# A feed-forward stage with its operands exchanged: exact sign weights in two products, scale and bias per partition, and transposes back

## What is computed

```python
x = layernorm(x + attention(x, Wq, Wk, Wv))
w = (weights >= 0.0) * 2.0 - 1.0              # +1 or -1, 512 x 512
y = einsum('bsi,oi->bso', x, w)
y = clip(y * scale + bias, -100, 100)          # scale, bias: (512,)
x = layernorm(x + y)
```

## Time and profile before

| | |
|---|---|
| median of 3 runs | 2723.28 us (2723.14 to 2724.53) |
| the profiled execution | 2723.15 us |
| its span in the profile | 2721.4 us |
| PE busy | 2686.9 us (99%) |
| DVE busy | 2308.4 us (85%) |
| ACT busy | 2261.1 us (83%) |
| POOL busy | 341.1 us (13%) |

### The profile page before, as it was taken

The page is one execution under the profiler, slowest core; times in us unless marked ns, Lnnn a source line. Parts: engine busy times, 40 slices in busy tenths (PEclk is TensorE's granted clock), DMA queues, the critical chain, the costliest instruction groups (busy, mean ns, idle before and its releaser), DMA issues.

```text
span 2721.4 us, 76294 instructions
## 1 busy us (share of the span) xinstructions
PE 2686.9 (99%) x32088; PEld 1351.0 (50%) x32088; DVE 2308.4 (85%) x1983; ACT 2261.1 (83%) x2726; POOL 341.1 (13%) x342
## 2 busy tenths in 40 slices
PE   9999999999999999999999999999999999979998
PEld 8888888733333333333333333333333333337887
DVE  7444444389999999999999999999999999978998
ACT  5333333399999999999999999999999999965665
POOL 1000000000000000010000000000000000005665
PEclk9999999999999999999999999999999999989999
DMA  6555555557686777768677686867768677655553
GB/s 227 191 194 193 188 186 186 197 132 169 132 176 140 155 157 158 162 126 184 138 153 165 142 172 135 167 147 157 168 131 172 141 159 158 150 145 177 189 189 136
DMA packets 216706, 445.22 MB, mean 164 GB/s; under 512 B 15570, under 2 KB 130258, under 8 KB 189780
## 3 DMA queue, kind: packets, MB, share of 16 engines
q0 software_dynamic: 27504, 200.29, 37.4%
q1 hardware_dynamic: 179108, 222.61, 26.2%
q10 hardware_dynamic: 9792, 17.83, 1.7%
HBM read 122.43 MB, written 117.96 MB: 88 GB/s over the span
## 4 chain that ended last, share of the span: by engine, by line
ACT 48%; PE 31%; issue 16%; DMA 3%; DVE 2%; SPq 0%; DVEq 0%; POOL 0%; ACTq 0%; POOLq 0%
ACT probs L769 48%; PE banks L226 19%; PE banks L1007 7%; DMA total<-partial 2%; PE banks L632 1%; PE banks L996 1%; PE banks L661 1%; PE banks L989 1%; PE banks L1003 1%; DVE partial L818 1%; DVE total L821 0%; DVE partial L821 0%; PE banks L248 0%; PE banks L990 0%; PE banks L254 0%
## 5 line engine op out<-in xcount | busy, mean ns | idle before, releaser
L769 ACT ACTIVATE probs<-banks 128x1024 f32<-128x1024 f32 x2048 | 1877.7, 1457 | 3.9 <-PE banks L632 3.9
L632 PE MATMUL banks<-score_rows 97*32 97x512 f16 x16384 | 1117.4, 380 | 4.5 <-issue 4.0
L661 PE MATMUL banks<-probs,v_keys 128*32 128x512 f32 x8192 | 1060.5, 592 | 0.1
L821 DVE TENSOR_TENSOR partial<-partial,probs 128x2048 f32<-128x2048 f32 x384 | 879.4, 2290 | 33.4
L632 PEld LDWEIGHTS banks<-score_rows 97*32 97x32 f16 x16384 | 361.3, 95 | 708.2 <-ACT probs L769 484.3
L818 DVE TENSOR_TENSOR partial<-probs 128x2048 f32<-128x2048 f32 x192 | 439.6, 2290 | 23.6 <-ACT probs L769 16.7
L601 POOL DMA_DIRECT2D total<-partial x191 | 164.7, 862 | 1713.7 <-DMA total<-partial 703.3
L661 PEld LDWEIGHTS banks<-probs,v_keys 128*32 128x32 f32 x8192 | 249.0, 111 | 209.9 <-ACT probs L769 0.2
L821 DVE TENSOR_TENSOR total<-total,probs 128x2048 f32<-128x2048 f32 x128 | 292.6, 2286 | 6.8
L354 DVE TENSOR_TENSOR qk_lo<-banks,qk_hi 128x512 f16<-128x512 f32 x128 | 88.3, 690 | 241.6 <-ACT qk_hi L309 241.6
L680 PEld LDWEIGHTS banks<-total,ones 128*32 128x32 f32 x3584 | 105.6, 109 | 280.7 <-issue 265.1
(11 more groups left out here) (95 smaller groups left out, 2117.5 us busy)
## 6 DMA issues: line engine op xcount, KB each, us to landing
total<-partial POOLq DMA_DIRECT2D x191, 1024.0 KB, 8.3
scratch_q_raw<-qk_raw SPq DMA_DIRECT2D x16, 1024.0 KB, 5.7
scratch_k_raw<-qk_raw SPq DMA_DIRECT2D x16, 1024.0 KB, 5.7
scratch_v<-v_out SPq DMA_DIRECT2D x16, 1024.0 KB, 5.1
score_rows<-scratch_q_hi SPq DMA_DIRECT2D x128, 128.0 KB, 4.6
score_rows<-scratch_k_hi SPq DMA_DIRECT2D x128, 128.0 KB, 3.5
v_keys<-scratch_v SPq DMA_DIRECT2D x64, 256.0 KB, 5.8
scratch_attn<-wf_scaled SPq DMA_DIRECT2D x64, 256.0 KB
```

The source lines that it names most:

```text
L632: last = nc.tensor.matmul(scores_of(phase, unit)[part, i, :], k_rows[:, h, keys], q_rows[:, h, qb * BLK:(qb + 1) * BLK], start=True, stop= ...
L661: last = nc.tensor.matmul(banks[rows, out_bank(qb), :], v_keys[:, kt, rows], probs[:, kt % P_RING, h, :], start=(kt == 0), stop=(kt == KT ...
L769: nc.scalar.activation(probs[:, kt % P_RING, heads, :], scores_of(it % SLOTS, qb * UNITS + u), ACT.Exp, scale=SCALE / GAIN ** 2).then_inc( ...
L821: nc.vector.tensor_tensor(into, into, probs[:, kt % P_RING], ALU.add).then_inc(a_sum, 1)
```

## The change

The feed-forward product is turned round. The sign weights, which are exactly representable, become the stationary operand `wf`, unscaled and unsplit; the moving operand is `yT` of four tiles (512 tokens). One unit u is then one group of 128 output features for 512 tokens: four chunks times two parts, 8 products of 512 columns where there were 13. The result has features in partitions, so ScalarE applies scale and bias as a column each while it evicts (`linear`), GpSimd clips (`clipped`), and TensorE transposes each tile back with four transposes (lag `BACK` = 11), from which VectorE adds y (`res2`).

The lags grow to `LN1, TRANS, FFN, LINEAR, BACK, LN2 = 1, 2, 6, 7, 11, 12`, so that the 64 tiles take 76 steps. `y` gets 16 slots, in the room of the score rows. The denominators are no longer transposed tile by tile: three batches in 16 transposes at the start of the block, the last one in 16 more in step 5, with their reciprocals in groups (`reciprocal_of`). `std`, `rstd` and `offset` are made once for both normalisations of a step, `offset` now from two tensors. On TensorE a step is: transposes of `y` (j-2), of `attnT` (j), back (j-11), product (u = j-6). On VectorE it begins with `res2` (j-11). The stores of the output go to SyncE's queue. The first loads of the block (`den`, `attnT`, and now x) are issued ahead of the last item's stores. Loops written as hardware loops become unrolled. In `project` the scaled and split weights and the bias rows go away. Of the diff, cut to its core:

```diff
--- project
-                nc.vector.scalar_tensor_tensor(out=wf_scaled[:], in0=w_in[:, 3], scalar=-1.0,
-                                               in1=scale_b.unsqueeze(1).to_broadcast([P, DC, D]),
-                                               op0=ALU.add, op1=ALU.mult).then_inc(s_scaled, 1)
-                nc.vector.tensor_copy(bias_rows[0:1, :], bias_in[0:1, :]).then_inc(s_bias, 1)
-                nc.vector.tensor_copy(bias_rows[HD:HD + 1, :], bias_in[HD:HD + 1, :]).then_inc(s_bias, 1)
...
-                nc.vector.tensor_tensor(wf_lo[:], wf_scaled[:], wf_hi[:].bitcast(FP32), ALU.subtract).then_inc(s_wflo, 1)
+                nc.vector.tensor_scalar(wf[:], w_in[:, 3], -1.0, None, ALU.add).then_inc(s_sign, 1)
...
--- attend
-    out_sb, den_sb = wf_scaled[:, 0:2, :], wf_scaled[:, 2:4, :]
+    out_sb = sb("out_sb", [P, 2, BLK], FP32)
+    den_sb = sb("den_sb", [P, 2, BLK], FP32)
...
+        def first_loads():
             for h in range(2):
+                sp.wait_ge(a_store[h], LAST * QB // 2 * 32 + 32)
+            sp.dma_start(first.den[:], dram["den"][0:(N - 1) * H, :]).then_inc(first.s_den, 16)
+            sp.dma_start(first.attnT[:], dram["attn"][0, :, 0:BLK].rearrange("(c p) t -> p c t", p=P)).then_inc(first.s_attnT, 16)
+            sp.dma_start(first.x[:], x[0]).then_inc(first.s_x, 16)
...
+            first_loads()
             for qb in range(QB):
                 store(LAST, qb)
-            finish_stores()
...
--- normalise_and_ffn
-    ATTN, LN1, TRANS, FFN, CLIP, LN2 = 0, 1, 2, 4, 5, 6
+    LN1, TRANS, FFN, LINEAR, BACK, LN2 = 1, 2, 6, 7, 11, 12
+    STEPS = TILES + LN2
...
     def _(sp):
+        for j in range(STEPS + 1):
+            if j % TPB == 0 and 2 <= j // TPB + 1 < NBLK:
+                load(j // TPB + 1)
+            t = lagging(j - 1, LN2)
+            if t is not None:
+                sp.wait_ge(f_y[1], t + 1)
+                sp.dma_start(out[t], y2[:, t % 4]).then_inc(f_out[t % 4], 16)
...
     def _(pool):
-                nc.gpsimd.tensor_tensor(res2[:, s % 2], clipped[:, s % 2], y[:, s % Y_SLOTS], ALU.add).then_inc(f_res[1], 1)
+            u = lagging(j, LINEAR)
+            if u is not None:
+                q, o = divmod(u, DC)
+                pool.wait_ge(f_linear, u + 1)
+                if q >= 2:
+                    pool.wait_ge(f_back, (q - 1) * TPB)
+                nc.gpsimd.tensor_scalar(clipped[:, q % 2, o, :], linear[:, u % 2, :], -MAX_VAL, MAX_VAL, ALU.max,
+                                        ALU.min).then_inc(f_clip, 1)
...
     def _(pe):
+        pe.wait_ge(first.s_den, 16)
+        rows = (N - 1) * H
+        for kt in range(KT):
+            last = nc.tensor.transpose(banks[:, 4 + kt // 8, kt % 8 * rows:(kt % 8 + 1) * rows],
+                                       first.den[:, kt * P:(kt + 1) * P], ident3[0:rows, 0:rows])
+        last.then_inc(f_denT, 1)
+        for j in range(STEPS):
+            t = lagging(j, TRANS)
             if t is not None:
+                pe.wait_ge(f_y[0], t + 1)
+                if t >= 2:
+                    pe.wait_ge(f_ylo, t - 1)
                 for c in range(DC):
+                    last = nc.tensor.transpose(yT_bank(t)[:, c * P:(c + 1) * P], y[:, t % Y_SLOTS, c * P:(c + 1) * P], ident3[:])
+                last.then_inc(f_yT, 1)
+            t = lagging(j, 0)
...
+                    last = nc.tensor.transpose(aT_bank(t)[:, c * P:(c + 1) * P], attnT[k][:, c, cols], ident3[:])
+                last.then_inc(f_aT, 1)
+            t = lagging(j, BACK)
             if t is not None:
...
+                    pe.wait_ge(f_clip, (q + 1) * DC)
+                if t >= 2:
+                    pe.wait_ge(f_res[1], t - 1)
+                for o in range(DC):
+                    last = nc.tensor.transpose(back_bank(t)[:, o * P:(o + 1) * P], clipped[:, q % 2, o, cols], ident3[:])
+                last.then_inc(f_back, 1)
+            if j == FFN - 1:
+                pe.wait_ge(f_denlast, 16)
+                for kt in range(KT):
+                    last = nc.tensor.transpose(banks[:, 6, kt * H:(kt + 1) * H], den_last[:, kt * P:(kt + 1) * P],
+                                               ident3[0:H, 0:H])
+                last.then_inc(f_denT, 1)
+            u = lagging(j, FFN)
+            if u is not None:
+                q, o = divmod(u, DC)
...
+                if o == 0:
+                    pe.wait_ge(f_ylo, (q + 1) * TPB)
+                if u >= 2:
+                    pe.wait_ge(f_linear, u - 1)
                 for c in range(DC):
-                    for part, w in ((yT_hi, wf_hi), (yT_lo, wf_hi), (yT_hi, wf_lo)):
+                    for part in (yT_hi, yT_lo):
+                        last = nc.tensor.matmul(ffn_bank(u), wf[:, c, o * P:(o + 1) * P], part[:, q % 2, c, :],
+                                                start=(c == 0 and part is yT_hi), stop=(c == DC - 1 and part is yT_lo))
                 last.then_inc(f_ffn, 1)
...
     def _(act):
+            if u is not None:
+                o = u % DC
+                act.wait_ge(f_ffn, u + 1)
...
+                nc.scalar.activation(linear[:, u % 2, :], ffn_bank(u), ACT.Identity, scale=columns[:, 0, o:o + 1],
+                                     bias=columns[:, 1, o:o + 1]).then_inc(f_linear, 1)
...
+                nc.scalar.activation(std[:, j % 2, lanes], mean_var[:, j % 2, lanes, 1], ACT.Sqrt, bias=eps[:]).then_inc(f_std, 1)
+            t = lagging(j, LN1)
             if t is not None:
+                act.wait_ge(f_offset, j)
...
+                nc.scalar.activation(y[:, t % Y_SLOTS], res1[:, t % 2], ACT.Identity, scale=rstd[:, j % 2, 0:1],
+                                     bias=offset[:, j % 2, 0:1]).then_inc(f_y[0], 1)
...
     def _(dve):
+        for j in range(STEPS):
+            t = lagging(j, BACK)
             if t is not None:
+                dve.wait_ge(f_back, t + 1)
...
+                nc.vector.tensor_tensor(res2[:, t % 2], back_bank(t), y[:, t % Y_SLOTS], ALU.add).then_inc(f_res[1], 1)
+            norms = norms_at(j)
+            for which, t in norms:
+                dve.wait_ge(f_res[which], t + 1)
+                nc.vector.bn_stats(stats[:, j % 2, which], (res1, res2)[which][:, t % 2]).then_inc(f_stat[which], 1)
...
+                nc.vector.reciprocal(rstd[:, j % 2, lanes], std[:, j % 2, lanes]).then_inc(f_rstd, 1)
+                dve.wait_ge(f_rstd, j)
+                nc.vector.scalar_tensor_tensor(out=offset[:, j % 2, lanes], in0=mean_var[:, j % 2, lanes, 0], scalar=-1.0,
+                                               in1=rstd[:, j % 2, lanes], op0=ALU.mult, op1=ALU.mult).then_inc(f_offset, 1)
...
```

More of the change, by code:

```diff
@@ L62, in project @@
 def project(nc, ctx, dram, args, banks, ffn, early):
-    xT, WT, WfT, scale, bias = args
-    wf_hi, wf_lo, bias_ones, bias_rows, wf_scaled = ffn
+    xT, WT, WfT, scale_bias = args
+    wf, columns = ffn
     rows16, v_keys, v_out = early.rows16, early.v_keys, early.v_out
@@ L154, in _ @@
         sp.dma_start(w_in[:, 3], WfT).then_inc(s_wf, 16)
-        sp.dma_start(scale_b, scale.partition_broadcast(P)).then_inc(s_ffn, 16)
-        for row in (0, HD):
-            sp.dma_start(bias_in[row:row + 1, :], bias.partition_broadcast(1)).then_inc(s_ffn, 16)
+        sp.dma_start(columns[:], scale_bias).then_inc(s_columns, 16)
         for b in range(NBLK):
@@ L546, in _ @@
             store(LAST, QB - 1)
-            finish_stores()
+            for h in range(2):
+                sp.wait_ge(a_store[h], ITEMS * QB // 2 * 32 + 32)
+            first_loads()
         with sp.Else():
@@ L588, in _ @@
                                 pattern=[[-1, P]], channel_multiplier=1).then_inc(m_id, 1)
-        pool.wait_ge(a_const, 1)
-        nc.gpsimd.memset(first[1][:], 0.0).then_inc(a_const, 4)
         pool.sem_inc(m_max, 2)
@@ L863, in normalise_and_ffn @@
     mean_var = sb("mean_var", [P, 2, 2, 2], FP32)
-    std = sb("std", [P, 2, 2, 1], FP32)
-    rstd = sb("rstd", [P, 2, 2, 1], FP32)
-    offset = sb("offset", [P, 2, 2, 1], FP32)
+    std = sb("std", [P, 2, 2], FP32)
+    rstd = sb("rstd", [P, 2, 2], FP32)
+    offset = sb("offset", [P, 2, 2], FP32)
     f_const = sem("f_const")
-    f_den = sem("f_den")
-    f_in = [first[2], sem("f_in1")]
-    f_x = [sem(f"f_x{k}") for k in range(2)]
+    f_denlast = sem("f_denlast")
+    f_denT = sem("f_denT")
+    f_rden = sem("f_rden")
+    f_in = [first.s_attnT, sem("f_in1")]
+    f_x = [first.s_x, sem("f_x1")]
     f_aT = sem("f_aT")
-    f_rden = sem("f_rden")
     f_attn = sem("f_attn")
@@ L1009, in step @@
                 last.then_inc(f_ffn, 1)
-        all_steps(pe, step)
     @block.scalar
     def _(act):
-        act.sem_inc(f_y[0], 2)
-        act.sem_inc(f_y[1], 2)
-        def deviation(t, s, which):
-            act.wait_ge(f_stat[which], (t + 1) * 2)
-            act.wait_ge(f_rstd[which], (t + 1) * 2)
-            nc.scalar.activation(std[:, s % 2, which], mean_var[:, s % 2, which, 1:2], ACT.Sqrt, bias=eps[:]).then_inc(f_std[which], 1)
```

(27 more changed lines are left out.)

343 lines of the change are left out of this document (146 added, 197 removed).

## The result

The median is **2900.7 us** (4 runs, 2898.8 to 2901.5) against 2723.2 us before (4 runs): ratio 1.0646, interval 1.0633 to 1.0659. The profiled execution's span is 2899.5 us. It is slower, as forecast, and inside the range, but 36 us above the predicted 2865.

The account below looks back on a forecast made before the run. TensorE was taken to bound the kernel at 4.02 us a tile. Start to 2489.6, 55 loop steps of 5.58 us (307) and the end gave 2827 us at full clock; 38 for alternating clock made 2865, range 2815 to 2985.

Parts of the forecast that it names:

- The loop: Last stage, each step: offset, ScalarE's y, TensorE's three transpose groups, VectorE's res2 to the next offset, in 55 steps.
- The 5.58 us: Length of one turn of the loop at full clock, summed from its members, against 4.02 us a step before.
- The likeliest case: TensorE's clock alternates, half of the time at each level: 6.27 us a step, 2865 us, chance 0.40.
- The 0.69 us for the clock: Step's lengthening by alternating clock, from 5.58 to 6.27 us; fully at the low level it would be 1.38.
- 38 us were put down for the clock: Last stage: the alternating clock adds 38 us to the full-clock 2827 us, giving 2865.
- The rival "`offset` behind GpSimd's addition": VectorE's two-tensor offset waits for GpSimd's res1: 1.27 us a step more, 2909 us at full clock; chance 0.26.
- The race of 0.04 us: After attn starts, GpSimd's res1 would start at 0.77 us and VectorE's offset at 0.81; first to start decides.
- The start: Last stage before the full loop: TensorE starts at 2442.64, den transposes 3.5 us, reciprocals 0.7; ends at 2489.6.
- At nothing, under the exponentials: Attention stage: issuing the first loads ahead of the last item's stores was costed at nothing, hidden under the exponentials.
- The clip: GpSimd's clip of 512 elements, with no row to size it, taken as 1.29 us like its addition.
- VectorE alone, 2.4 a step: End of the last stage: ten steps without transposes of y, 2.4 us each on VectorE with std between, 24 us.
- The rival on the other side: If y reaches TensorE in time, no loop: VectorE's 3.5 us sets the step, 2713 us; chance 0.06.

Follow-up runs that it names:

- e12: Changed kernel with offset made by one tensor-and-column operation per normalisation and every feed-forward product made twice: 2841.7 us, 5.60 us a step.
- e2: Changed kernel with TensorE's step reordered: transposes back first, then of attnT, then of y, then the product: 2816.9 us.
- e1: Changed kernel with offset made, as before the change, by one operation of a tensor and a column for each normalisation: 2848.0 us.
- e4: Changed kernel with each feed-forward product made twice into the same bank, the second overwriting the first: 2878.9 us.
- e5: Changed kernel with the first loads of den, attnT and x issued behind the last item's four stores instead of ahead: 2901.6 us.
- e9: e8 with the three first loads issued one by one, each ahead of one of the last three stores: 2735.0 us.
- after: The kernel with the whole change and no follow-up edit, against the kernel before: 2900.7 us, ratio 1.0646.
- e8: e3 with four slots for res2 in place of two: 2735.7 us.
- e10: e9 with GpSimd's addition res1 ahead of its clip in each step: 2768.1 us.
- e3: Changed kernel with the edits of both e1 and e2, offset by columns and transposes back first: 2782.6 us.
- e13: e10 with transposes back and the last normalisation each a step later (lags 12 and 13): 2711.8 us.
- e7: Kernel before the change with eight products instead of twelve, the weights' low part left out: 2705.7 us.
- e11: e10 with 8 unread products of 512 columns added in each of steps 1 to 5 of the last stage: 2765.5 us.

## Why the prediction was right, and where it was off

**The loop: right.** The chain has its members in the predicted order, VectorE's `res2` is released by the transposes back and TensorE's transposes by `y`. The 5.58 us were 5.60 in `e12`, at full clock and without a held `offset`, and opening the loop (`e2`) took 84 us off. The terms one by one, from the turn shown: `res2` to `attn` 2.02 (2.10 predicted), `attn` to `rstd` 0.59 (0.61), `rstd` to `offset` 0.19 (0.20), `y` and the wait of TensorE 0.86 (0.87), the transposes until `res2` 1.57 (1.49).

**The likeliest case: its kind right, its size off, and a rival missing in it.** The clock did alternate, but less: it was 0.85 and not the 0.75 of half and half. In 23 of the 52 steps from 12 to 64 the transposes of the loop ran at the low level (17 of these steps took over 7.7 us, 5 behind a free `offset` 6.57 to 6.72, the last 6.87), and a step at the low clock cost 1.28 more and not 1.38. The 0.69 us for the clock were 0.54, and 0.23 in the version in columns (`e1`). That 38 us were put down for the clock and about 28 came is a size that was off, not a wrong mechanism. The step of the working that failed is to leave `offset` at its old cost in the likeliest sum, as if either the clock or the hold would come and not both. The rival "`offset` behind GpSimd's addition" (chance 0.26) came true *besides* the clock: `offset` to `y` was 1.30 and not 0.31, in 40 of those 52 steps. `e1` takes 53 us off, `e12` against `e4` 37. That the likeliest number still came within 36 us of the result is in part luck: it had too much for the clock and nothing for the hold. The rival itself was 2909 at full clock, 5.58 + 1.27 = 6.85 us a step; `e4`, at full clock, has 6.28 and 2879. There the turn with a free `offset` takes 5.43, a hold adds 1.11, and each fourth `offset` starts first. The race of 0.04 us that the prediction named was decided by 0.02 to 0.03 us, against `offset` in three steps of four. The Trainium skill (SBUF — State Buffer, "SBUF: two separate sides") gives this rule, the first to start locks the other out for the whole instruction. The trace agrees for `offset`: 1.26 us behind the addition, 0.16 ahead of it. It does not show the other half: an addition that started 0.03 to 0.04 us behind `offset` lasted 1.26 to 1.28 us, as any other, and not the 0.12 to 0.13 longer that waiting for `offset` to end would add.

**The sum of 36 us.** Step 12's `offset` stood at 2505.85; predicted at 6.27 a step 2489.6 + 2 x 6.27 = 2502.1: 3.7 late. The 52 steps behind it took 0.55 more each (6.82 against 6.27): 28.8. The step to 2865.11 took 4.4 and not 6.27: 1.9 off. From there to the end of the span 34.4 and not 28.4: 6.0, which is mostly the wait for `res2`'s slot. The median lies 1.2 us above the profiled span, where 1.75 were added: 0.5 less. Together 36.1.

**The start.** Three terms were mis-sized, and the first two partly cancel: 16 transposes of `den` 1.94 us (3.5 predicted; they move only 48 columns), the two reciprocals 1.77 (0.7), and TensorE started at 2447.04 and not at 2442.64. It waited there for GpSimd's `ident`, behind an attention stage that ended 7 us later. "At nothing, under the exponentials" was wrong for the first loads: they account for 4.2 of those 7 us (`e5`), though at most some 3 us of it reach the end of the kernel (`e9`).

**The clip.** 1.92 us and not 1.29. In after it hid in the loop, where GpSimd is idle for about half of the step. It mattered only when the loops were gone (`e8`, `e10`).

**What was overlooked.** The second loop, over `res2`'s two slots: 4.79 us a step (`e3`), hidden under the first and worth 47 us when it was alone. And "VectorE alone, 2.4 a step" for the end, where it showed already.

**The rival on the other side.** "No loop", 2713 us with VectorE's 3.5 us a step, was rightly put at 0.06 for this change. `e13` is that case: 3.65 us and 2711.8. It took six edits to get there, and what it gains on the kernel before is of the size that `e7` gained by relieving TensorE alone (19 us), since VectorE is next in both (3.79 us a step there).

**What stays open.** What the burst of first loads costs the whole kernel (0 to 3 us, `e9`), why the attention stage of after ends 2.8 us late even without it, and what a start at the high clock is worth (`e11`): all three are near what these runs can tell. Nor does any run take the hold of `offset` away by other means than its form, such as a later addition on GpSimd in every step.

## What to carry to other kernels

Before counting what an engine saves, walk once around the new order: if an engine's first operation in a step needs another's result that in turn needs its own last operation of the step before, the sum of that circle is the step, and moving one group of instructions (84 us here) or adding buffer slots (47 us) can be worth more than the operations saved (19 us in `e7`). When one circle is opened, look for the next longer wait (a slot count, the order on a third engine, a lag of one step) before judging the idea: here the same operations ran in 2901 and in 2712 us. And a tiny operation with two tensors in SBUF on VectorE should not stand on such a circle just where GpSimd starts a long one.

## What the hardware showed unexpectedly

- A 128x2 operation of VectorE with two tensors took 0.16 us or 1.26 us, by whether it started 0.03 us before or 0.02 us after GpSimd's addition; with one tensor and a column the same values took two operations and 0.33 us beside it.
- Twice the products on TensorE made the kernel 22 us faster (2900.7 to 2878.9), and the granted clock was then 1.00 instead of 0.86 (2520 to 2680).
- GpSimd needed 1.92 us for a clip of one tensor of 128x512 with two constants, more than for its addition of two such tensors (1.26 to 1.30).
- VectorE's reciprocal of 128x128 out of PSUM took 0.88 us, more than a two-tensor operation on 128x512 (0.69).
